# Layer 0's future-key mask for the row maxima: from TensorE products to an add-and-maximum on VectorE

## The reference, cut to what matters

```
att = einsum('bhqd,bhkd->bhqk', q, k) / scale
att = where(tril(ones((t, t))), att, -inf)   # a query sees no later key
att = softmax(att, axis=-1)
y = einsum('bhqk,bhkd->bhqd', att, v)
```

## Time and profile before

| | |
|---|---|
| three runs | 1531.5, 1529.0, 1526.57 us |
| median | 1529.0 us |
| span of the profiled execution | 1526.1 us (which of the three times is its own is not marked; the lowest is 0.5 us above it) |
| mean granted TensorE clock | 0.974 |
| busy: TensorE, VectorE, ScalarE, GpSimd | 94%, 71%, 52%, 53% |

### The profile page before, as it was taken

The page is one execution under the profiler, slowest core; times in us unless marked ns, Lnnn a source line. Parts: engine busy times, 40 slices in busy tenths (PEclk is TensorE's granted clock), DMA queues, the critical chain, the costliest instruction groups (busy, mean ns, idle before and its releaser), DMA issues. The chain is left out here.

```text
span 1526.1 us, 32899 instructions
## 1 busy us (share of the span) xinstructions
PE 1430.0 (94%) x12438; PEld 1054.5 (69%) x12438; DVE 1077.7 (71%) x2040; ACT 801.1 (52%) x1135; POOL 809.4 (53%) x1002
## 2 busy tenths in 40 slices
PE   5788989899999999999999999999999999999997
PEld 3555657667676767677776777777777777777676
DVE  7779686778787787785556658657677486575866
ACT  2444444343444443546656666666666556666652
POOL 4233535254443534444757667656666675766552
PEclk8899999899999999999999999999999999999999
DMA  5111120212121111220100001100100101000000
GB/s 190 61 60 57 56 70 23 84 42 83 42 83 42 56 54 57 84 70 17 47 29 1 1 1 43 43 2 2 43 1 1 43 1 43 1 1 29 2 29 15
DMA packets 45763, 61.34 MB, mean 40 GB/s; under 512 B 3760, under 2 KB 31312, under 8 KB 45648
## 3 DMA queue, kind: packets, MB, share of 16 engines
q1 hardware_dynamic: 44784, 59.03, 11.4%
q10 hardware_dynamic: 864, 0.66, 0.1%
HBM read 25.83 MB, written 8.39 MB: 22 GB/s over the span
## 5 line engine op out<-in xcount | busy, mean ns | idle before, releaser
L1720 ACT ACTIVATE l_probs<-psum 128x1024 f32<-128x1024 f32 (+1 forms) x192 | 164.4, 880 | 139.3 <-PE psum L2048 115.6
L912 ACT ACTIVATE l_probs<-psum 128x512 f32<-128x512 f32 x256 | 138.1, 594 | 177.3 <-PE psum L1179 174.7
L994 DVE TENSOR_REDUCE l_rowmax<-psum 128x2 f32<-128x1024 f32 (+2 forms) x192 | 159.1, 863 | 41.3 <-PE psum L1140 41.0
L310 POOL TENSOR_SCALAR_AFFINE_SELECT l_probs<-l_probs 128x256 f32<-128x256 f32 (+1 forms) x384 | 182.6, 506 | 0.0
L305 POOL TENSOR_TENSOR l_pool_holder<-expo 128x1 f32<-128x1 f32 x128 | 31.0, 242 | 270.8 <-ACT l_probs L1726 178.2
L1816 DVE TENSOR_TENSOR l_qk_lo<-psum,l_qk_hi 128x1024 fp32r<-128x1024 f32 x64 | 78.0, 1218 | 135.2 <-ACT l_qk_hi L1710 134.8
L1726 ACT ACTIVATE l_probs<-l_probs 128x2048 f32<-128x2048 f32 (+1 forms) x128 | 161.8, 1268 | 0.7
L2091 PE MATMUL psum<-l_probs,l_v 128*32 128x512 f32 (+3 forms) x2048 | 151.1, 434 | 2.1 <-DVE l_att L1838 2.1
L1825 DVE RECIPROCAL l_keysum<-psum 128x256 f32<-128x256 f32 x64 | 112.2, 1753 | 52.4 <-PE psum L2077 51.1
L1838 DVE TENSOR_TENSOR l_att<-psum,l_keysum 64x256 f32<-64x256 f32 x256 | 108.0, 422 | 23.6 <-PE psum L2091 14.1
L2091 PEld LDWEIGHTS psum<-l_probs,l_v 128*32 128x32 f32 x2048 | 64.6, 110 | 84.2 <-issue 72.9
(11 more groups left out here) (239 smaller groups left out, 4174.8 us busy)
## 6 DMA issues: line engine op xcount, KB each, us to landing
l_kT<-l_roped_hi SPq DMA_DIRECT2D x32, 256.0 KB, 2.5
l_qT<-l_roped_hi SPq DMA_DIRECT2D x32, 256.0 KB, 2.6
l_xin<-in_x SPq DMA_DIRECT2D x8, 512.0 KB, 4.5
l_kT<-l_roped_lo SPq DMA_DIRECT2D x16, 256.0 KB, 2.8
l_qT<-l_roped_lo SPq DMA_DIRECT2D x16, 256.0 KB, 2.5
l_x<-in_x SPq DMA_DIRECT2D x8, 512.0 KB, 4.0
x_mid<-l_x SPq DMA_DIRECT2D x8, 512.0 KB, 3.1
l_xin<-x_mid SPq DMA_DIRECT2D x8, 512.0 KB, 4.2
```

The costliest lines, as they stand in the source:

```text
L310: nc.gpsimd.affine_select(out=part, in_=part, compare_op=ALU.is_ge, fill=0.0, base=0, pattern=[[0, part.shape[1]], [1, P]], channel_multip ...
L912: space.free(nc.scalar.activation(probs[:, SLOT[p], e, c0:c1], space.unit(*use), ACT.Exp, scale=HD0 ** -0.5), *use)
L994: reduced = nc.vector.tensor_reduce(rowmax[:, a // 2, :, a % 2, t], space.unit("max", a, k)[:, :, c0:c0 + (t + 1) * P], mybir.AxisListType ...
L1720: space.free(nc.scalar.activation(probs[:, p % 2, :, c0:c1], space.unit("score", p, u)[:, :, 0:c1 - c0], ACT.Tanh, scale=HD1 ** -0.5 / CLA ...
```

## The change

The mask products go. VectorE adds the mask itself: a new constant `hidden_keys` (128 x 512, float32) is zero but for its last 128 columns, which hold -1e30 where the key is later than the query. For each tile and head, one `tensor_tensor_reduce` reads the scores from PSUM and the last (t + 1) x 128 columns of `hidden_keys`, writes the sums back over the scores and the maximum of them to `rowmax`. Ahead of each unit a `memset` of one column carries the unit's wait. Unit by unit the order of pieces on every engine stays as it is. The counts of the waits inside the loop are found in another way (`repeated`, the largest over the batches that the loop runs, with `back` for waits on the batch before).

```diff
-    later = sb("later", [P, P], BF16)
-    rows_of = sb("rows_of", [P, 2, P], BF16)
+    hidden_keys = sb("hidden_keys", [P, T])
+    max_holder = sb("max_holder", [P, 3 * PAIRS])
...
+    def repeated(self, b, use, numbers, share, back):
+
+        if isinstance(b, int):
+            return numbers[use, b]
+        return max(numbers[use, c - back] - (c - back) * share for c in self.schedule.batches() if (use, c - back) in numbers)
...
-            count = self.linear(b, use, self.fill_number[use, self.known(b, use)], self.full_share[use[0]])
+            count = self.repeated(b, use, self.fill_number, self.full_share[use[0]], back)
...
+        nc.gpsimd.memset(hidden_keys[:], 0.0).then_inc(consts, 1)
...
+        nc.gpsimd.affine_select(out=hidden_keys[:, T - P:T], in_=hidden_keys[:, T - P:T], compare_op=ALU.is_ge, fill=MASKED, base=0,
                                 pattern=[[-1, P]], channel_multiplier=1).then_inc(consts, 1)
...
+        def seen_max(scores, a, e, t):
+            keys = (t + 1) * P
+            return nc.vector.tensor_tensor_reduce(scores, scores, hidden_keys[:, T - keys:T], 1.0, LOWEST, ALU.add, ALU.max,
+                                                  rowmax[:, a // 2, e, a % 2, t:t + 1])
+
         def row_max(i, a, k):
             space.filled(dve, i, "max", a, k)
+            nc.vector.memset(max_holder[:, 2 * a + k:2 * a + k + 1], 0.0)
             for t, c0 in MAX_UNITS[k]:
-
-                reduced = nc.vector.tensor_reduce(rowmax[:, a // 2, :, a % 2, t], space.unit("max", a, k)[:, :, c0:c0 + (t + 1) * P],
-                                                  mybir.AxisListType.X, ALU.max)
+                for e in range(2):
+                    reduced = seen_max(space.unit("max", a, k)[:, e, c0:c0 + (t + 1) * P], a, e, t)
             space.free(reduced, "max", a, k)
...
             for t, c0 in MAX_UNITS[k]:
-                max_tile(unit, a, t, c0, c0 == 0)
-            for t, c0 in MAX_UNITS[k]:
-                last = later_keys(unit, c0 + t * P, (t, c0) == MAX_UNITS[k][-1])
+                last = max_tile(unit, a, t, c0)
             space.fill(last, "max", a, k)
```

More of the change, by code:

```diff
@@ L108, in round @@
             if piece[0] in pieces:
+                self.issued = piece
                 pieces[piece[0]](j - self.shift[piece], *piece[1:])
@@ L118, in loop, with batches @@
                 self.round(j, pieces)
+    def batches(self):
+        shift = self.shift[self.issued]
+        return range(self.lo - shift, self.hi - shift + 1)
     def uses(self, *names):
@@ L765, in place @@
                 scores = [("score", p, k, 1) for p in half for k in range(len(PAIR_UNITS))]
-                space.all_filled(sp, i - 1, scores + [("tail", p // 2, 1) for p in half])
+                space.all_filled(sp, i - 1, scores + [("tail", p // 2, 1) for p in half], back=1)
             sp.wait_ge(rope_high.sem, high)
@@ L787, in load_x @@
             if started(i):
-                space.all_filled(sp, i - 1, [("x_T", b) for b in range(NT // 2)])
+                space.all_filled(sp, i - 1, [("x_T", b) for b in range(NT // 2)], back=1)
                 sp.dma_start(xin[:], tok(a["x"], i)).then_inc(x_loaded.sem, 16)
@@ L1128, in placed_rows, with max_tile @@
                 pe.wait_ge(which.sem, which.at(i, PLACED * (a // 4 + 1)))
-        def max_tile(unit, a, t, c0, first):
+        def max_tile(unit, a, t, c0):
             for e in range(2):
                 rows = slice(ROW0 * e, ROW0 * e + KLAST)
[L1133 to L1141, removed]
+                last = nc.tensor.matmul(unit[:, e, c0:c0 + (t + 1) * P], qT[rows, a, t * P:(t + 1) * P],
+                                        kT[rows, a, 0:(t + 1) * P], start=True, stop=True)
             return last
@@ L1160, in row_max_tail @@
             for n in range(2):
-                max_tile(unit, 2 * g + n, MAX_TAIL, n * wide, n == 0)
-            for n in range(2):
-                last = later_keys(unit, n * wide + MAX_TAIL * P, n == 1)
+                last = max_tile(unit, 2 * g + n, MAX_TAIL, n * wide)
             space.fill(last, "max_tail", g)
@@ L1632, in keys @@
                 before, q = earlier(i, p)
-                space.freed(pool, before, "pv", q)
+                space.freed(pool, before, "pv", q, back=int(p < 2))
             else:
@@ L1707, in projected @@
                 if started(i):
-                    space.all_filled(act, i - 1, [("score", p - 2 + NP1, u) for u in range(len(UNITS1))])
+                    space.all_filled(act, i - 1, [("score", p - 2 + NP1, u) for u in range(len(UNITS1))], back=1)
                 space.filled(act, i, "qk", p)
@@ L1822, in den @@
                 before, q = earlier(i, p)
-                space.freed(dve, before, "pv", q)
+                space.freed(dve, before, "pv", q, back=int(p < 2))
             space.filled(dve, i, "den", p)
```

54 lines of the change are left out of this document (21 added, 33 removed).

## The result

The changed kernel takes 1536.55 us (median of 4 runs, 1535.98 to 1536.99) against 1528.3 us for the kernel before on the same chip: ratio 1.0047, 95% interval 1.0031 to 1.0062. It is slower by some 8 us, where 22 were forecast (1551 us). Direction and range were right, the size was not.

A forecast was written before the change was run, and what follows sets the result against it. VectorE was taken to bound each round's first stage, TensorE the second. VectorE's +3.9 us less TensorE's 1.2 gave +2.7 per round, +22 us over eight batches: 1551 us, 8-in-10 range 1512 to 1600.

The forecast's parts named there:

- units of the first stage: Eight of a layer 0 round's 20 units, in the stretch where VectorE was taken to set the pace.
- The bound by stage: Layer 0 round, 361 to 442 us: VectorE sets the pace in 361 to 391, TensorE in 391 to 442.
- The rival in which VectorE's addition hides throughout: Whole round: TensorE sets the end, 1.9 to 3.7 us per round won, 1509 us; chance 0.17.
- VectorE in the first stage: Longer units plus 26 instructions of 0.10 us add 1.3 + 2.6 = 3.9 us per round, all counted.
- d: Extra time of an add-and-maximum over a plain addition on VectorE: 0.10 us taken, bounds 0.01 to 0.21.
- VectorE in the second stage: Stretch 391 to 442 us: 5.7 us more VectorE work per round fits 13.5 us of idle time, costing nothing.
- The batches outside the loop: Batches built outside the loop were taken to have dense stretches like it: +2.7 us each, eight batches +22 us.
- TensorE's saving: Dropped mask products save 2.0 us per round (1.9 to 3.7); only the second stage's 12/20 counts, 1.2, at most 2.2.
- the 0.09 us given back per unit: Float32 weight loads (186 ns against 95), no longer covered by mask products, in 20 units: saving 3.7 down to 1.9 us.
- The signs I had named: If right: first stage 30 to about 34 us, TensorE idle there 8 us, second about 50 us, layer 1 unchanged.
- a fully VectorE-bound round: Rival: VectorE's in-order queue bounds the whole round, up to 9.6 us per round, 1606 us; chance 0.16.
- The cheap instruction: Rival: the add-and-maximum costs 0.01 to 0.03 us over an addition, about 1530 us; chance 0.15.

The follow-up runs named there:

- 0.9979: Changed kernel with mask products and plain reductions put back in the eight units of the first stage, add-and-maximum in the other 12; against the kernel before: 1526.31 us.
- 1.0076: Kernel before with add-and-maximum only in the eight units of the first stage, mask products kept everywhere: 1540.44 us, +11.6 us.
- +8.0: Changed kernel with the 12 units outside the first stage put back to mask products and plain reductions: 1537.45 us, ratio 1.0052 to the kernel before.
- the vector part alone: Changed kernel with TensorE's mask products kept in all batches (mask added twice): 1546.3 us, ratio 1.0126 to the kernel before.
- the tensor part alone: Mask products dropped, VectorE's plain reductions kept, so maxima leave the mask out: 1517.45 us, ratio 0.9923 to the kernel before.
- the fastest kernel: Mask products dropped only in the 12 units outside the first stage, plain reductions everywhere (mask left out of those maxima): 1513.67 us, ratio 0.9905 to the kernel before.

## Why the prediction was off, by its own steps

All totals below are forecast per round times eight, beside the measured difference of two kernels.

| step | forecast | measured |
|---|---|---|
| VectorE, units of the first stage | +31 us | +11.6 (8.7 to 14.5) |
| VectorE, the 12 other units | 0 | +11.3 (0.9979 less 0.9905) or +7.6 (1.0126 less 1.0076), each within some 4 |
| TensorE, the 12 other units | -10 us | -14.5 (-17.9 to -11.2) |
| TensorE, units of the first stage | 0 | -3.6 (+8.0 less 11.6), +2.7 (-11.8 plus 14.5): none that can be told |
| sum | +22 us | +7.2 (4.7 to 9.5) |

**The bound by stage: half right.** VectorE's work in the first stage does cost, and TensorE's in the second pays. The rival in which VectorE's addition hides throughout (1509 us) is out: the vector part alone costs 19 us.

**VectorE in the first stage: the largest step that failed.** "Together +3.9 us where VectorE has 1.3 us of idle time": measured +1.5 us of busy time per round and +1.4 us of time (11.6 / 8). The term was mis-sized twice over. First, its price. The units leave (1.26 - 2 x 0.59) / 2, (1.49 - 2 x 0.65) / 4 and (1.49 - 4 x 0.33) / 4 over the forecast's additions, so d was 0.04 to 0.05, not 0.10 (for 512 elements it can't be told from nothing: 0.61 us, beside 0.61, from 394.44 to 395.05, for the subtraction of the same size in the same trace); and the memset ahead of each unit, taken at 0.06, cost nothing. I had read small instructions behind small ones and put their distance behind long ones, where none stood. The Trainium skill, VectorE: DVE Perf Modes, section Two Vector instructions with no wait between them, has the accumulator read as an instruction of its own: the trace agrees, 512 of them at 141 ns. It was my inference that each would also take its time in the queue that the trace refutes. Second, its passing on in full: by unit rows the stage had to get 3 x 0.13 + 3 x 0.30 + 2 x 0.36 = 2.0 us, and at the same clock it grew by 0.8, since at 0.87 VectorE had 2.5 us of idle time there and not 1.0. The rest of the 1.4 us fits the clock, which reached 1.00 in no stage with the new work: a stage of 24.3 us at 1.00 is one of 25.9 at 0.87. That VectorE's longer work lowers the clock is likely from the count of stages, but no run isolates it.

**VectorE in the second stage: another step that failed.** "5.7 us of VectorE work go into 13.5 us of idle time and cost nothing." The work was 2.9 to 3.4 us, and about a third of it, 0.8 to 1.0 us per round (56.2 against 55.4, 54.9 against 53.9), reached TensorE. VectorE's idle time is an average; a unit's banks are held longer each time, and where their next owner was due at once, TensorE stopped, as behind tail 0. I had named this ("a unit that is released later holds its banks longer") and priced it only in the first stage. It is spread: with the largest wait taken away and that unit's products put back, the stage stayed at 55.0 us.

**The batches outside the loop: the third.** "I take the batches outside the loop to have dense stretches like it." Batch 0 does not: the same 12 units that cost 0.8 to 1.0 us in a second stage cost 5.6 to 6.2 us in it. That is half or more of what they cost in all.

**TensorE's saving: mis-sized.** 1.2 us per round were forecast, up to 2.2 at its end; busy time in the second stage fell by 1.7 (54.38 to 52.70), the stage of the tensor part alone by 1.4 (55.3 to 53.9), and the total by 14.5 / 8 = 1.8. The difference between 1.4 and 1.8 is not a second stage's: the trace of the fastest kernel has three of its four first stages at full clock, 24.2 or 24.3 us long, the first trace before only one, though the products in them are the same. So the 0.09 us given back per unit for the float32 weight loads seems too much; where these loads lie was not measured by itself.

**The signs I had named.** The first stage did not grow to 34 us: by the cut used here it was 24.3 to 26.0 us before and 25.4 to 26.6 after. TensorE idles 5.5 us in the one of 25.4, against 4.5 in the one of 24.3, not 8. The second did not lose 1.2 us but 0.3. TensorE's waits for VectorE in the second stage, which I had given to the rival of a fully VectorE-bound round (1606 us), did come, though only 1.1 us of them. The cheap instruction (1530 us, d up to 0.03) was nearer than my value, 6.5 us below the measured time where the forecast is 14.5 above, but by luck in part: it too costs the second stage at nothing and passes the first stage's work on in full.

The errors cancelled in part: 20 us too much in one term, 8 to 11 us missing in the next, 5 us too little saved. With the first stage's 11.6 and TensorE's 14.5 right and the rest still at nothing, the sum would have been -3 us: that the direction came out right is in part luck.

**What stays open.** That batch 0 holds more than its share is shown, and so is the engine, VectorE; but the 3.1 and 1.0 us of longer waits for maxima there are not the whole of the 6 us, and I did not follow the rest. The shift at batch 1 is in part the scatter of single traces: done the old way, batch 1 ended at 211.4, 215.1 and 216.7 us in three of them, at a clock of 0.87, 0.84 and 0.84 over the first 130 us. How much of VectorE's price passes through a lower clock stays open too.

## What to carry to other kernels

Idle time of an engine covers new work only if the buffers it holds are not due: here about a third of the work put into it came out as time. Before you price work at nothing, look at who takes the bank next and how long after the release. Move the work where its receiver is waiting anyway and leave it where it sets the pace: here the change in 12 units of 20 gave -3 us, in all 20 it gave +7. Price an instruction by the distance to its neighbour of the kind it will really stand beside. And look at the batches outside a loop by themselves: the first one need not have the loop's idle time.

## What the runs showed of the hardware that I had not expected

- A one-column memset on VectorE runs beside the long instruction ahead of it: it starts 0.02 to 0.07 us after that one's start, and 512 of them (59 ns each) cost 3 us in all. The accumulator read (132 to 152 ns) starts with the following instruction. With the read and the sums written back to PSUM, an add-and-maximum of 512 elements takes 0.61 or 0.65 us in the queue, where the subtraction of 512 elements takes 0.59 before and 0.61 in the same trace.
- The same first stage of the same kernel ran at a granted clock of 0.82, 0.87 and 1.00 in one trace, 28.1, 25.9 and 24.3 us long. A comparison of single stages has to be made at the same clock. At the same clock they repeat: 24.2 or 24.3 us in all nine at 1.00, in four kernels.
